# A decoder layer pair on one core: an output projection and the next cross attention's projections put into one block, in chunks

## The reference

```python
x = layernorm(x + self_attention(x) @ w_out.T)            # ends with the projection "Do"
Q = rope((x @ Wq.T + bq) per head)                        # 512 queries per batch
K = rope((ctx @ Wk.T + bk) per head)                      # 1601 keys per batch
V = (ctx @ Wv.T + bv) per head
scores = where(mask == 0, -big, Q @ K.T / 4)
x = layernorm(x + softmax(scores) @ V @ Wo.T + bo)        # ends with the projection "Eo"
```

## Time and profile before

| what | us |
| --- | --- |
| median of 3 runs | 2354.23 (2348.57 to 2354.61) |
| the profiled execution | 2346.18 |
| its span | 2344.4 |
| busy in the span: PE / DVE / ACT / POOL | 1955.6 / 1418.4 / 1022.4 / 496.6 |
| start of `Do`, first DMA issue | 1366.20 |
| start of the `E_` block | 1405.70 |
| first DMA issue of the heads of cross attention | 1568.72 |
| start of `Eo` | 2143.16 |

### The profile page before, as it was taken

How to read it: one execution, slowest core, us unless ns; L and a number is a source line. 1 busy time by engine, 2 the same in 40 slices (tenths; PEclk the granted TensorE clock), 3 DMA queues, 4 the chain that set the end, 5 groups by cost and what they waited for, 6 DMA issues and landing times. The chain is left out here.

```text
span 2344.4 us, 31585 instructions
## 1 busy us (share of the span) xinstructions
PE 1955.6 (83%) x12024; PEld 1115.2 (48%) x12024; DVE 1418.4 (61%) x2456; ACT 1022.4 (44%) x1595; POOL 496.6 (21%) x670
## 2 busy tenths in 40 slices
PE   8879588887499999957799975867999999998696
PEld 4777355555388888844233342531222222223454
DVE  1431243334457777764578735769999999983523
ACT  1110132333055565521266731113788888885320
POOL 1420000000135555420433114240111111100100
PEclk9999799999599999977699988985999999998699
DMA  3000545554456666622211006430110111100201
GB/s 112 1 1 1 218 168 203 203 198 155 157 228 259 237 273 244 245 86 96 64 29 35 16 5 226 163 105 13 30 29 16 30 30 30 30 1 7 75 0 36
DMA packets 100637, 237.47 MB, mean 101 GB/s; under 512 B 27438, under 2 KB 71090, under 8 KB 96888
## 3 DMA queue, kind: packets, MB, share of 16 engines
q1 hardware_dynamic: 76092, 200.53, 23.4%
q0 software_dynamic: 23872, 31.71, 5.0%
q10 hardware_dynamic: 528, 3.28, 0.3%
HBM read 180.19 MB, written 54.69 MB: 100 GB/s over the span
## 5 line engine op out<-in xcount | busy, mean ns | idle before, releaser
L1431 DVE TENSOR_REDUCE Eh_maxima<-Eh_max 128x2 f32<-128x802 f32 x512 | 474.9, 987 | 31.1 <-PE Eh_max L1316 26.1
L1419 ACT ACTIVATE Eh_probs<-Eh_pair 128x1024 f32<-128x1024 f32 (+1 forms) x288 | 287.8, 999 | 127.3 <-PE Eh_pair L1355 127.0
L805 PE MATMUL C_y<-C_x_high,C_W 128*128 128x256 f16 x1472 | 250.2, 274 | 1.5 <-DVE C_x_low L1051 1.5
L1316 PE MATMUL Eh_max<-Eh_KS,Eh_QS 49*128 49x401 f16 x1024 | 197.8, 357 | 56.4 <-DVE Eh_maxima L1431 39.8
L1378 PE MATMUL Eh_av_ps<-Eh_probs,E_V 128*17 128x512 f32 (+1 forms) x1664 | 224.1, 611 | 0.1
L805 PE MATMUL C_y<-C_x_low,C_W 128*128 128x256 f16 x736 | 201.4, 274 | 0.0
L1431 DVE TENSOR_REDUCE Dh_maxima<-Dh_max 128x2 f32<-128x1024 f32 x128 | 152.1, 1221 | 51.0 <-PE Dh_max L1324 49.0
L1419 ACT ACTIVATE Eh_probs<-Eh_single 128x512 f32<-128x512 f32 x272 | 161.5, 594 | 19.0 <-PE Eh_single L1355 18.8
L1316 PEld LDWEIGHTS Eh_max<-Eh_KS,Eh_QS 49*128 49x128 f16 x1024 | 50.4, 94 | 245.1 <-DVE Eh_maxima L1431 196.8
L805 PEld LDWEIGHTS C_y<-C_x_high,C_W 128*128 128x128 f16 x1472 | 144.6, 98 | 18.9 <-issue 1.9
L1355 PE MATMUL Eh_pair<-Eh_QS,Eh_KS 51*128 51x512 f16 (+1 forms) x560 | 118.5, 393 | 11.1 <-ACT Eh_probs L1419 10.5
(11 more groups left out here) (323 smaller groups left out, 3508.7 us busy)
## 6 DMA issues: line engine op xcount, KB each, us to landing
C_W<-w_split SPq DMA_DIRECT2D x23, 3072.0 KB, 11.4
S_w<-in_w_experts_dram SPq DMA_DIRECT2D x32, 768.0 KB, 8.6
w_split<-S_parts SPq DMA_DIRECT2D x32, 768.0 KB, 5.9
Eh_KS<-E_kd POOLq DMA_DIRECT2D x64, 150.1 KB, 3.3
C_tail<-in_expert_tail_dram SPq DMA_DIRECT2D x23, 384.0 KB, 8.3
B_ctxT<-in_ctxT_dram SPq DMA_DIRECT2D x4, 1601.0 KB
E_ctxT<-in_ctxT_dram SPq DMA_DIRECT2D x4, 1601.0 KB, 12.3
B_ctxN<-in_ctx_dram SPq DMA_DIRECT2D x4, 1536.0 KB
```

Source lines behind the costliest of these rows:

```text
L805: last = mm(y_ps[n % Y_BANKS][:, i, :], W[:, u, a, at_w:at_w + P], x[:, s % 2, k, :], start=(q == 0), stop=(q == len(parts) - 1))
L1316: last = self.nc.tensor.matmul(bank[:, a, 0:self.cw], self.QS[r, slot, p, qt * P:(qt + 1) * P], self.KS[r, slot, p, k0:k0 + self.cw], star ...
L1419: self.nc.scalar.activation(dst, src, ACT.Exp, scale=1.0 / SCORE).then_inc(self.exp_done, 1)
L1431: self.nc.vector.tensor_reduce(self.maxima[:, g % 2, :, p * TPB + qt, c], self.max_ps[n % 2][:, :, 0:self.cw], AX_X, ALU.max).then_inc(sel ...
```

## The change

- `project_out` becomes a class, `OutProjection`. The first transposes no longer wait for the weights. Products go in pairs of tiles into two PSUM tensors `Do_out` (two banks, a ring of 2), and DVE adds a pair with one instruction.
- `Do` runs inside the `E_` block. Its parts stand on each engine ahead of the items, except that PE does key items 0 and 1 between the last product and turning back, and ACT their value copies. `renew_semaphores` now stands between the heads of self attention and this block.
- Keys come first and queries last. Key chunks are 384, 384, 384 and 449 columns, numbered 0 to 15 over the four batches, queries 16 to 19. Context is loaded by chunk into a ring of 4, the mask by chunk into a ring of 2, the rotary tables in 4 pieces, the weights with semaphores of their own.
- Work is shared out anew. The multiplication by `keep` or by the query scale goes from DVE to POOL (one instruction for both halves), the value copies and the mask's row go from DVE to ACT, and ACT's cast and POOL's subtraction are one instruction per item. The hardware loops are written out.
- The value bias leaves the value copies. It goes through the last projection instead: `Eo` adds `bv @ Wo.T + bo` to the residual, which costs a small product and one addition.

```diff
-def project_out(nc, ctx, name, X, XT, ATT, ident, WoT, bo):
...
-            pe.wait_ge(loaded, need)
...
+class OutProjection:
...
+        attended(0)
+        pe.wait_ge(self.loaded, self.need)
+        if self.bias is not None:
+            for k in range(KD):
+                last = mm(self.out_ps[0][:, 0, :], self.bv[:, k:k + 1].broadcast_to([P, P]), self.W[:, k, :], start=(k == 0), stop=(k == KD - 1))
+            last.then_inc(self.shift_ready, 1)
+            pe.wait_ge(self.bias_ready, 1)
+        for c in range(B):
+            if c + 1 < B:
+                attended(c + 1)
+            project(c)
+
...
+    def tensor_back(self, pe):
+        pe.wait_ge(self.copied, KD * B)
+        for c in range(B):
+            turn_group(self.nc, pe, self.X, self.ident[:], self.turn_ps, c, self.norm.normed, self.copied_back, self.turned_back)
...
+    def vector(self, dve):
+        v = self.nc.vector
+        if self.bias is not None:
+            dve.wait_ge(self.shift_ready, 1)
+            v.tensor_tensor(self.bo[:], self.out_ps[0][:, 0, :], self.bo[:], ALU.add).then_inc(self.bias_ready, 1)
+            dve.wait_ge(self.bias_ready, 1)
+            for c in range(B):
+                x = self.X[:, c * TPB:(c + 1) * TPB, :]
+                v.tensor_tensor(x, x, self.bo[:].rearrange("p (a d) -> p a d", a=1).broadcast_to([P, TPB, D]), ALU.add).then_inc(self.based, 1)
...
-    with ExitStack() as own:
-        project_out(nc, own, "Do", X, XT, ATT, ident, dram["self_WoT"], None)
...
+KEY_CHUNK = 3 * P
...
+    KC = S2 // KEY_CHUNK
+    CW = S2 - (KC - 1) * KEY_CHUNK
+    starts = [c * KEY_CHUNK for c in range(KC)]
+    widths = [KEY_CHUNK] * (KC - 1) + [CW]
+    KEYS = B * KC
+    ITEMS = KEYS + B
+    RING = 4
...
-                for b in range(B):
-                    query(b, b % 2, b // 2)
-                for b in range(B):
-                    sp.wait_ge(row_half, b + 1)
-                    sp.wait_ge(row_ready, b + 1)
-                    sp.dma_start(mask_rows[b], mask_row[:, b % 2]).then_inc(row_stored[b % 2], 16)
-                    if b + 1 < B:
-                        load_mask(b + 1)
-                    for c in range(KC):
-                        key(b, b % 2, c % 2, b * (KC // 2) + (B // 2 + c // 2), c)
-                    if b + 2 < B:
-                        sp.wait_ge(keys_done, b + 1)
-                        load_context(b + 2, b % 2)
...
+                def load_mask(n):
+                    b, c0, w, _ = part_of(n)
+                    if n >= 2:
+                        sp.wait_ge(keep_ready, n - 1)
+                    sp.dma_start(mask[:, n % 2, 0:w], dram["mask"][b, :, c0:c0 + w]).then_inc(mask_loaded[n % 2], 16)
...
+                after.sync(sp)
+                for x, n in ((wk, "wkT"),):
+                    sp.dma_start(x[:], dram[n].rearrange("(k p) e -> p k e", p=P)).then_inc(wk_loaded, 16)
+                sp.dma_start(bk[:], dram["bk"]).then_inc(wk_loaded, 16)
+                load_context(0)
+                sp.dma_start(wv[:], dram["wvT"].rearrange("(k p) e -> p k e", p=P)).then_inc(wv_loaded, 16)
+                for c in range(KC):
+                    load_turns(c)
+                    if c < 2:
+                        load_mask(c)
+                    if c + 1 < RING:
+                        load_context(c + 1)
+                sp.dma_start(wq[:], dram["wqT"].rearrange("(k p) e -> p k e", p=P)).then_inc(wq_loaded, 16)
+                sp.dma_start(bq[:], dram["bq"]).then_inc(wq_loaded, 16)
+                for n in range(ITEMS):
+                    b, c0, w, keys = part_of(n)
+                    if 1 <= n < KEYS - RING + 1:
+                        load_context(n - 1 + RING)
+                    if 1 <= n < KEYS - 1:
+                        load_mask(n + 1)
+                    if keys:
+                        sp.wait_ge(row_ready, n + 1)
+                        sp.dma_start(mask_rows[b, :, :, c0:c0 + w], mask_row[:, n % 2:n % 2 + 1, 0:w].broadcast_to([1, 2, w])).then_inc(row_stored[n % 2], 16)
+                    sp.wait_ge(low_ready, n + 1)
+                    dst, first, last = (kd, slice(0, 4), slice(4, 6)) if keys else (qd, slice(2, 6), slice(0, 2))
+                    u = slice(b * H, (b + 1) * H)
+                    for m in range(2):
+                        both = slice(first.start + m, first.stop, 2)
+                        sp.dma_start(dst[both, u, :, c0:c0 + w].rearrange("g u d s -> (u d) g s"), parts[:, n % 2, m, :, 0:w]).then_inc(stored[n % 2][m], 16)
+                        sp.dma_start(dst[last.start + m, u, :, c0:c0 + w].rearrange("u d s -> (u d) s"), parts[:, n % 2, m, 0, 0:w]).then_inc(stored[n % 2][m], 16)
+                for i in range(2):
+                    sp.wait_ge(row_stored[i], 16 * (KEYS // 2))
+                    for m in range(2):
+                        sp.wait_ge(stored[i][m], 32 * (ITEMS // 2))
...
+                def key(n):
+                    pe.wait_ge(ctx_loaded[n % RING], 16 * (n // RING + 1))
+                    project(n)
+                    for i in ops_of[n]:
+                        b, c, kts = value_ops[i]
+                        if i < 2:
+                            pe.wait_ge(after.sum_ready, NT // 2)
+                        else:
+                            pe.wait_ge(v_copied, i - 1)
+                        for q, kt in enumerate(kts):
+                            r, at = key_rows(kt), kt * P - starts[c]
+                            for k in range(KD):
+                                last = mm(v_ps[i % 2][0:r, q, :], ctxT[:, n % RING, k, at:at + r], wv[:, k, :], start=(k == 0), stop=(k == KD - 1))
+                        last.then_inc(v_product, 1)
+                    pe.wait_ge(v_product, ops_of[n][-1] + 1)
+                    pe.sem_inc(chunk_read, 1)
+
+                after.tensor(pe)
+                pe.wait_ge(wk_loaded, 32)
+                pe.wait_ge(wv_loaded, 16)
+                key(0)
+                key(1)
+                after.tensor_back(pe)
+                for n in range(2, KEYS):
+                    key(n)
+                pe.wait_ge(wq_loaded, 32)
+                pe.wait_ge(after.copied_back, KD * B)
+                for n in range(KEYS, ITEMS):
+                    project(n)
...
+                def values(n):
+                    for i in ops_of[n]:
+                        b, c, kts = value_ops[i]
+                        r, k0 = key_rows(kts[-1]), kts[0]
+                        act.wait_ge(v_product, i + 1)
+                        for q, kt in enumerate(kts):
+                            o = nc.scalar.activation(V[0:r, kt, b * H * VW:(b + 1) * H * VW].rearrange("p (h v) -> p h v", v=VW)[:, :, 0:DH],
+                                                     v_ps[i % 2][0:r, q, :].rearrange("p (h d) -> p h d", d=DH), ACT.Copy)
+                        o.then_inc(v_copied, 1)
...
+                after.scalar(act)
+                values(0)
+                values(1)
+                after.scalar_back(act)
+                for n in range(ITEMS):
+                    if n < KEYS:
+                        row(n)
+                        if n >= 2:
+                            values(n)
+                    high(n)
...
-                nc.gpsimd.memset(V[:], 1.0).then_inc(v_ones, 1)
...
+                def lower(n):
+                    w = part_of(n)[2]
+                    pool.wait_ge(high_ready, n + 1)
+                    tt(parts[:, n % 2, :, 1, 0:w], t[:, n % 2, :, 0:w], parts[:, n % 2, :, 0, 0:w], ALU.subtract).then_inc(low_ready, 1)
+
+                pool.wait_ge(scale_ready, 1)
+                for n in range(ITEMS):
+                    _, _, w, keys = part_of(n)
+                    factor = keep[:, n % 2:n % 2 + 1, 0:w] if keys else query_scale[:].rearrange("p (a s) -> p a s", a=1)
+                    pool.wait_ge(summed, n + 1)
+                    tt(t[:, n % 2, :, 0:w], t[:, n % 2, :, 0:w], factor.broadcast_to([P, 2, w]), ALU.mult).then_inc(kept, 1)
+                    if n >= 1:
+                        lower(n - 1)
+                    pool.wait_ge(kept, n + 1)
+                lower(ITEMS - 1)
...
-                def query(b, u, turn):
-
-                    rotate(u, turn, bq, 0, S, lambda t: v.tensor_scalar(t, t, 0.25 * SCALE, None, ALU.mult))
...
-                def key(b, u, slot, turn, c):
-                    c0, w = chunks[c]
-                    rotate(slot, turn, bk, c0, w, lambda t: v.tensor_tensor(t, t, keep[:, u, c0:c0 + w], ALU.mult))
-                    for kt in v_tiles[c]:
-                        r = key_rows(kt)
-                        dve.wait_ge(v_product, b * NK2 + kt + 1)
-                        v.tensor_tensor(V[0:r, kt, ds(b * H * VW, H * VW)].rearrange("p (h v) -> p h v", v=VW)[:, :, 0:DH],
-                                        v_ps[kt % 4][0:r, :].rearrange("p (h d) -> p h d", d=DH),
-                                        bv[0:r, :].rearrange("p (h d) -> p h d", d=DH), ALU.add).then_inc(v_copied, 1)
...
```

(20 more changed lines are left out.)

369 lines of the change are left out of this document (159 added, 210 removed).

## The result

The changed kernel takes **2424.4 us** (median of 4 runs, 2417.1 to 2431.2) against 2354.4 (4 runs, 2348.6 to 2356.5): a ratio of 1.030, with an interval of 1.026 to 1.034. Its profiled execution took 2427.9 us, with a span of 2426.1. The forecast was 2420 (2397 to 2448).

The account below looks back on a forecast made before the run. PE and DVE shared the bound before; afterwards a loop through the mask load decides. Block 267.7 us, plus 1.5 later start, less the old 202.5, less 1 in `Eo`: +65.7 us, giving 2420 (2397 to 2448).

Parts of the forecast that it names:

- the later start: Joined block: it begins some 1.5 us later than before, because `renew_semaphores` moves ahead of it.
- The whole ring: Key items: mask load waits behind SP's stores, those for POOL, POOL for DVE, DVE for the mask; 12.8 us per item.
- The start: Block's beginning: products end at +20.9 us, key items 0 and 1 at +32.2, turning back at +43.0.
- The sum of item 2: DVE's sum of key item 2, the first with a late mask, ready at +55.1 us from the block's start.
- The turn: From one key item's sum to the next, no steps overlapping: 12.8 us, thirteen times from item 2 to item 15.
- the landing: The mask's way in, 192 KB behind 384 KB of context: 3.3 us, bounds 2.1 and 6.4.
- the mask lands late: Rival, key items: landing 5.3 us instead of 3.3 gives 2448 us, at 6.4 gives 2463; chance 12%.
- Queries and the last POOL work: After the key items, DVE and POOL still take turns: 40.5 us, from +222.5 to +263.0.
- Costs put at nothing: PE's 5.5 us per item, ACT's copies and context loads: costed at nothing, as each fits under 12.8 us.
- The masks come in time: Rival, key items: masks land before POOL's subtraction ends, turn 7.07 us, kernel faster at 2342 us; chance 3%.
- PE is the bound: Rival, whole joined block: all chains hidden, PE's 149.5 us set the pace, -52.5, kernel 2302 us; chance 1%.
- Nothing else follows: Rival: early loads save the first part's wait, the rest keeps its pace, within 7 us of before; chance 2%.

Follow-up runs that it names:

- e1: Changed kernel with SP loading the mask of item n + 2 ahead of item n + 1's stores, not behind them: 2329.6 us, ratio 0.991.
- e2: Changed kernel with POOL subtracting each item right after multiplying it, not behind the next item's multiplication: 2332.6 us, ratio 0.992.
- e4: Changed kernel with the multiplication by keep or query scale moved back from POOL to DVE: 2320.4 us, ratio 0.987.
- e5: Changed kernel with masks in a ring of 4, loaded two items further ahead from the same place in SP's list: 2325.9 us, ratio 0.990.
- e7: Changed kernel with the edits of e5 and e4 together: 2302.7 us, ratio 0.979.
- e8: e7 with `Do` in a block of its own ahead of the `E_` block: 2319.3 us, ratio 0.986.
- e6: Changed kernel with the edits of e1 and e2 together: 2307.1 us, ratio 0.982.

## Why the prediction was right

**The total came closer than its parts.** Forecast were +65.7 us, and the medians differ by 70.0. The two profiled executions, which the sum was laid beside, differ by 81.7: the one before ran 8 us below its median and the changed one 3.5 above. Of the 16 us that the sum missed there, 8.2 are in the block, 5.8 in the heads of cross attention, which the sum had left out, and 2.6 in the later start, less 0.7 in `Eo`. So the agreement to 4 us is in part luck.

**The mechanism held at every step that it named.** DVE was idle before `E_keep` (L1919) 14 times, released by the DMA of `E_mask`, for 145.1 us or 10.4 each, where some 9 were expected. The whole ring is in one timeline, and e1, e2, e4 and e5 each loosened it at another place and took the time per item from 13.2 us to between 6.7 and 7.9. PE's granted clock fell to 0.75 in that stretch, as said. Its share there is 56%, above the half that I had put as a ceiling, for the reason that it runs slower: a record of PE takes 0.38 us in that stretch (99.59 over 264) and 0.26 in e7's at full clock (83.06 over 323).

**The start was on target, for the products and the two items.** The products ended at +21.6 where +20.9 was said, and the last copy of turning back ended about 1410.5, or +40.2; +43.0 was said. Two errors of opposite sign cancel in part. The transposes did not all start at once: the second group waited for `Do_W`, 1.46 us, because PE's list has the wait for the weights between the two groups. And turning back went faster, 7.5 us (1403.11 to about 1410.6) and not 10.8, since PE came out of two key items at the full clock and no longer waited for the norm:

```profile
1370.34 1.38 PE L1511 MATMUL Do_turn<-ident,attended 128*128 128x128 f32 x8 [2.28 <-PEq L2178]
1373.18 1.97 PE L1511 MATMUL Do_turn<-ident,attended 128*128 128x128 f32 x8 [1.46 <-DMA Do_W<-in_self_WoT_dram]
...
1403.11 1.06 PE L100 MATMUL Do_turn<-ident,X 128*128 128x128 f32 x8 [0.30 <-PE Do_out L1828]
...
1408.86 1.06 PE L100 MATMUL Do_turn<-ident,X 128*128 128x128 f32 x8 [0.83 <-ACT XT L108]
```

The sum of item 2 stood at +53.3, for +55.1. (The 2.4 us that the working puts between the old blocks are 1.8, from the end of the last copy at 1403.90; no term of the sum uses them.)

**The turn was mis-sized in one term, the landing.** The sum of item 2 to the sum of item 15 took 177.8 us (1423.63 to 1601.46), for 167.4. Of the terms of 12.8 us: the landing had 3.3 and measured 4.3 in the median (4.19 in the turn shown), +1.0; the multiplication had 1.8 and measured 1.6, -0.2; the subtraction (1.64), the four issues (1.95), the context's issue (0.50) and `keep` (0.36) were right. The two together are +0.8 in each of 13 turns, 10.4 us, and so the whole difference. Smaller ones cancel, among them one long issue (1.3 us over the usual), which no row of before suggested:

```profile
1526.17 1.78 SPq L1756 DMA_DIRECT2D E_ctxT<-in_ctxT_dram  x1
```

I had chosen `E_wv`, third of three loads of 256 KB in a row, as the nearest row. It was the nearest in size but not in company: this mask follows 384 KB of context and four stores. In the last two turns, with no context load in them, the landing is 3.0; the sum had taken 1.2 us off them, 0.48 for the issue and so 2.6 for the landing. The case "the mask lands late" had put 5.3; the truth lies between, and inside the loop's own range. By the Trainium skill, "DMA: Bandwidth & Descriptors", section "Anatomy of one DMA", which gives its formula for DMAs that GpSimd issues, the mask alone would take 2.45 us. SP issues this one, and the runs show the formula to be near even so: in e1 a mask of 384 columns that went alone (issued at 1398.86) landed in 2.4. In the changed kernel no landing is under 3.0.

**POOL's price was better by the row than by the rule.** POOL's multiplication of 128x768 takes 1.61 us where DVE's takes 0.96 in e4: 1.7 times. The doubling that the Trainium skill gives ("GPSIMD Engine Reference", section 4.1) is right in direction; it gives 1.92 from DVE's 0.96, an estimate; the working's 2.05 came from the two smaller instructions of before (1.07 us for two of 401 columns). What speaks against the move in this kernel is not POOL's speed, though. Moving it back in e4 saves 104 us, of which POOL's and DVE's difference in one turn (0.65 us, 16 times) is a tenth. Most of the rest is the place that the multiplication takes in POOL's list, as e2 shows, which leaves it on POOL and saves 92.

**The rest.** Queries and the last POOL work took 40.3 us (1601.46 to 1641.76), for 40.5. The tail from there to the next stage took 4.4 for 4.7. `Eo` saved 1.7 for 1.0. The block came to 275.9 for 267.7. Costs put at nothing stayed at nothing, with one exception: the first query waited 4.57 us for PE, whose granted clock was 0.72 then (1599.2 to 1606.1). That made its sum 0.6 us late, and POOL's multiplications of 1024, 2.12 us for 2.4, won it back: the 40.3 is a small piece of luck too.

**The rivals.** "The masks come in time" was priced at 2342 and had 3%. As a forecast of this change it fell; e5 makes it true and gives 2325.9, 16 us under the price. "PE is the bound" was priced at 2302, and e7, in which it is true, takes 2302.7. The items fit, 6.0 us each against the 5.5 and 5.7 of the working, but the agreement of the totals is luck: the block takes 158.6 us where 149.5 were said, and the median of before beside e7 was 4.4 us lower than the one that the price was added to. "Nothing else follows" does not apply: e7 against the changed kernel shows the key items in 108 us less (90.2 for 198.1), many times what the early start is worth (17 us in e8).

## What to carry to other kernels

When one engine issues both loads and stores, a load behind a store waits for all that the store waits for. Follow that chain through every engine's list until it ends, or comes back to the reader of the load. If it comes back, count how many items further on it arrives: the time per item is the sum of its steps divided by that count, and busy shares show only idle engines. Then change the count at the cheapest place (one place in a list, one deeper ring). From one item to two roughly halved the time per item here, wherever it was done, and DVE still waited for nearly every mask; from three on the next bound set the pace. Gains of two such edits do not add up.

## What the runs showed of the hardware that was not expected

**DVE and POOL held each other up, one whole instruction at a time.** `keep` (128x384, int32 to bf16) takes 0.36 us. Where it starts while an instruction of POOL's runs, it ends 0.21 to 0.27 us after POOL's, however early it began: so in all 26 cases of e1, e2, e4 and e6 in which 0.1 us or more of POOL's instruction was left. The timeline of DVE and POOL in e4:

```profile
1502.36 1.64 POOL L1894 TENSOR_TENSOR E_parts<-E_t,E_parts 128x768 f16<-128x768 f32 x1 [5.24 <-ACT E_parts L1871]
1502.50 1.72 DVE L1912 TENSOR_SCALAR E_keep<-E_mask 128x384 bf16<-128x384 int32 x1 [1.08 <-DMA E_mask<-in_mask_dram]
```

and the same two engines in e6, at three places:

```profile
1412.08 0.96 DVE L1942 TENSOR_TENSOR E_t<-E_t,E_other 128x768 f32<-128x768 f32 x1
1412.16 2.38 POOL L1894 TENSOR_TENSOR E_parts<-E_t,E_parts 128x768 f16<-128x768 f32 x1 [1.01 <-ACT E_parts L1871]
...
1439.72 1.65 POOL L1894 TENSOR_TENSOR E_parts<-E_t,E_parts 128x768 f16<-128x768 f32 x1 [1.01 <-ACT E_parts L1871]
1439.96 0.69 DVE L1936 SCALAR_TENSOR_TENSOR E_t<-E_pair,E_bk,E_rotary 128x449 f32<-128x449 f32 x1 [0.99 <-PE E_pair L1813]
...
1509.05 1.22 DVE L1942 TENSOR_TENSOR E_t<-E_t,E_other 128x1024 f32<-128x1024 f32 x1
1509.51 2.75 POOL L1894 TENSOR_TENSOR E_parts<-E_t,E_parts 128x1024 f16<-128x1024 f32 x1 [1.22 <-ACT E_parts L1871]
```

In e4 POOL was first, ended at 1504.00 as it would alone, and `keep` ended at 1504.22. In e6's first and last pair DVE was first and kept its time, and POOL's subtraction, 1.64 us alone, took 2.38, and the one of 1024, 2.12 alone, took 2.75: 0.74 and 0.63 us were added, nearly what was left of DVE's instruction (0.88 and 0.76 us). The sum of e7 and e4 at queries is the first case again: 1.69 us behind POOL, where it takes 1.22 alone. In between stands the exception: DVE's products run inside POOL's instruction and take the 0.68 that they take alone. They read PSUM and one tensor in SBUF; the sum reads two in SBUF. The Trainium skill ("GPSIMD Engine Reference", section 1, Specifications) says that GpSimd shares its SBUF interfaces with VectorE, with contention where a DVE instruction has two SBUF inputs or is in a 2-port mode. The sum and the products agree with that; which of `keep`'s properties puts it on the list no run here shows, though it is a fast one: each further 1000 columns cost it 0.53 us (0.36 for 384, 1.00 for the 1601 of the earlier trace rows), where they cost the sum 1.02 (0.96 for 768, 1.22 for 1024). What the rows add is the size: the later one waits, all but some 0.15 us, for the end of the earlier one. In the changed kernel the loop kept the two apart, and `keep` is never above 0.40; e1, e2, e4 and e6 pay up to 1.5 us in some items. In e2 and e4 that is 5 us over the key items, or 0.3 us an item, and accounts for about half of what their times per item (7.9 and 7.6) lie above the 7.3 and 7.0 expected.
